# A four-layer graph network on one core: scatter signals by half groups, later passes that use a chunk inside the next one's products, destination rows projected first

## The reference, cut to what matters

```python
# layer 0, twice: messages, gated update
agg = segment_sum(concat(h[src], h[dst]) @ W_msg.T + b_msg, dst)
gi, gh = agg @ W_ih.T + b_ih, h @ W_hh.T + b_hh
r, z = sigmoid(ir + hr), sigmoid(iz + hz); n = tanh(inn + r * hn)
h = where(deg > 0, (1 - z) * n + z * h, h)
# layer 1: weighted sum over edges, both ends normalised by degree
out = segment_sum(norm[:, None] * (h @ W)[src], dst) + b
# layer 2: attention per feature
e = leaky_relu((h @ W_src.T + b_src)[src] + (h @ W_dst.T + b_dst)[dst])
out = segment_sum((h @ W_v.T + b_v)[src] * edge_softmax(e, dst), dst)
# layer 3: mean over neighbours
h1 = relu(h @ W1 + b1); neigh = segment_sum(h1[src], dst) / max(deg, 1)
out = relu(relu(h1 @ W_self + neigh @ W_neigh + b_sage) @ W2 + b2)
```

## Time and profile before

| | us |
|---|---|
| median of 3 runs (lowest, highest) | 3011.63 (3008.87, 3012.08) |
| profiled execution, its own time | 3001.93 |
| its span | 3000.2 |
| scatters on POOL | 70.9 to 1085 |
| rest of unzip and first pass | 1085 to 1266 |
| pass 1 | 1266 to 1436 |
| pass 2 | 1461 to 1664 |
| to attention | 1664 to 1731 |
| attention | 1731 to 2749 |
| layer 3 with pass 3 | 2749 to 3000 |

### The profile page before, as it was taken

How to read it: one execution, slowest core, us unless ns; L and a number is a source line. 1 busy time by engine, 2 the same in 40 slices (tenths; PEclk the granted TensorE clock), 3 DMA queues, 4 the chain that set the end, 5 groups by cost and what they waited for, 6 DMA issues and landing times.

```text
span 3000.2 us, 36506 instructions
## 1 busy us (share of the span) xinstructions
PE 2037.3 (68%) x11168; PEld 1241.8 (41%) x11322; DVE 1720.4 (57%) x2673; ACT 977.4 (33%) x1778; POOL 1619.1 (54%) x1664
## 2 busy tenths in 40 slices
PE   4774006251615056899798389999999999994597
PEld 2222001021302024555444267666666666663244
DVE  7997412121212023535225279999999999997622
ACT  1000003120202020101200157777777777774101
POOL 1777777777777730020000467777777777775000
PEclk8555557665757578899999789999999999997799
DMA  9998979481835096442585389999999999995252
GB/s 388 375 367 320 366 255 393 171 294 30 291 121 187 3 304 191 145 154 68 204 284 165 110 249 314 313 309 304 301 316 310 313 307 310 312 306 180 88 177 64
DMA packets 496975, 724.17 MB, mean 241 GB/s; under 512 B 70532, under 2 KB 353725, under 8 KB 496880
## 3 DMA queue, kind: packets, MB, share of 16 engines
q1 hardware_dynamic: 425316, 608.72, 60.8%
q0 software_dynamic: 65680, 109.05, 12.3%
q10 hardware_dynamic: 5884, 5.21, 0.5%
HBM read 402.27 MB, written 320.51 MB: 241 GB/s over the span
## 4 chain that ended last, share of the span: by engine, by line
PE 31%; POOL 30%; issue 14%; DMA 12%; DVE 10%; ACT 1%; SPq 0%; POOLq 0%; DVEq 0%; ACTq 0%; another core or an unknown queue 0%
POOL adj_d L578 21%; POOL G L572 9%; DMA G<-tab_sv,src_e 8%; PE PS L911 7%; PE PS L920 5%; PE PS L647 3%; DMA G<-adj_d 3%; PE PS L941 2%; PE PS L936 2%; PE PS L966 2%; PE PS L781 2%; DVE V L1505 2%; PE PS L935 1%; DVE V L1504 1%; POOL run_d L616 1%
## 5 line engine op out<-in xcount | busy, mean ns | idle before, releaser
L578 POOL DMA_INDIRECT adj_d<-D,place x782 | 775.8, 992 | 303.2 <-issue 237.8
L572 POOL DMA_INDIRECT G<-tab_sv,src_e x784 | 758.8, 968 | 245.7 <-issue 220.0
L935 PE MATMUL PS<-ident,G 128*128 128x128 f32 x784 | 219.0, 279 | 110.1 <-DMA G<-tab_sv,src_e 63.4
L936 PE MATMUL PS<-VT 128*128 128x128 f32 x1568 | 274.9, 277 | 0.0
L1810 DVE TENSOR_TENSOR_SCAN RB<-mring,RB,PS 128x512 f32<-128x512 bf16 x196 | 249.3, 1272 | 23.9 <-PE PS L941 20.2
L1284 ACT ACTIVATE X<-G 128x512 f32<-128x512 f32 x150 | 98.8, 668 | 500.6 <-DMA G<-adj_d 500.6
L1790 DVE TENSOR_TENSOR_SCAN HTx<-PS,HTx,D 128x512 f32<-128x512 f32 x196 | 250.2, 1276 | 0.0
L1795 DVE TENSOR_TENSOR_SCAN ST<-PS,ST,M 128x512 f32<-128x512 f32 x196 | 250.0, 1276 | 0.0
L936 PEld LDWEIGHTS PS<-VT 128*128 128x128 f32 x1568 | 243.3, 196 | 0.0
L616 POOL DMA_INDIRECT run_d<-V,head_i x25 | 24.0, 959 | 382.3 <-ACT V L1354 375.0
L1175 ACT ACTIVATE OSF<-PS 128x512 f32<-128x512 f32 x392 | 209.9, 587 | 5.1 <-PE PS L647 3.8
(11 more groups left out here) (393 smaller groups left out, 4230.3 us busy)
## 6 DMA issues: line engine op xcount, KB each, us to landing
frac_d<-OSF SPq DMA_DIRECT2D x196, 512.0 KB
adj_d<-RB SPq DMA_DIRECT2D x7, 12800.0 KB, 74.1
G<-adj_d SPq DMA_DIRECT2D x162, 512.0 KB, 6.3
run_d<-RB SPq DMA_DIRECT2D x4, 12992.0 KB, 81.7
VT<-run_d SPq DMA_DIRECT2D x196, 256.0 KB
wts_d<-X SPq DMA_DIRECT2D x150, 256.0 KB, 6.5
mring<-cut_d SPq DMA_DIRECT2D x196, 128.0 KB
HTx<-seg_d SPq DMA_DIRECT2D x196, 128.0 KB
```

Source lines behind the costliest of these rows:

```text
L572: pool.indirect_dma_start(dest, None, table, bass.IndirectOffsetOnAxis(ap=idx, axis=0)).then_inc(done, 16)
L578: pool.indirect_dma_start(adj_d, bass.IndirectOffsetOnAxis(ap=place[:, 2 * w + k:2 * w + k + 1], axis=0), pay[:, w, k, :], None).then_inc( ...
L935: nc.tensor.matmul(o, G[:, h, k, 0:F], ident[:, :], is_transpose=True, start=k == 0, stop=False, skip_group_check=True)
L936: last = nc.tensor.matmul(o, GZ[:, h, k, :], HM[:, q, k * P:(k + 1) * P], start=False, stop=False, skip_group_check=True)
```

## The change

Four edits.

1. The scatter goes in 46 units of 9 and 8 windows in place of 23 groups of 17. In step u: writes k = 0 of unit u; wait for the k = 1 writes of unit u - 2 and `gdn` up; wait for the k = 0 writes of unit u - 1; its k = 1 writes. `gate_i` counts units.
2. Chunk 5 is unzipped in two pieces of 256 columns, as chunk 6 was, with two blocks to a load: 26 loads for 25. The work for earlier chunks goes with the first piece.
3. In the later passes chunk s - 1 is turned behind the fourth tile of chunk s and folded behind its twentieth, and its `after` comes at the end of chunk s. Behind the last chunk one turn, one fold and one `after` are left. ScalarE and VectorE follow. In pass 1, where only 5 tiles are left of chunks 0 and 1 in order, the turn stands behind the fourth of them and the fold behind the fifth.
4. Before attention the transposes of a group alternate with the product of its destination rows (128 columns), which ScalarE evicts at once; the source and value tables (256 columns) are a second round. SP stores all of `tab_d` before `tab_sv`. `MEV_L3` counts the 14 evictions.

```diff
-PIECES = [(j, 0, CW) for j in range(6)] + [(6, 0, 256), (6, 256, LASTC)]
+PIECES = [(j, 0, CW) for j in range(5)] + [(5, 0, 256), (5, 256, CW), (6, 0, 256), (6, 256, LASTC)]
-LOADS = [(i, b, 1 if j < 6 else min(2, NBR - b)) for ... for b in range(0, NBR, 1 if j < 6 else 2)]
+LOADS = [(i, b, 1 if j < 5 else min(2, NBR - b)) for ... for b in range(0, NBR, 1 if j < 5 else 2)]
+UW = (9, 8)
+NU = 2 * NSG
...
                 pool.wait_ge(gated, 1)
-                for g in range(NSG + 1):
-                    if g < NSG:
...
-                        for w in range(g * GW, (g + 1) * GW):
...
-                            issue(0, g, w)
-                    if g >= 1:
-                        landed(0, g - 1)
-                        for w in range((g - 1) * GW, g * GW):
-                            issue(1, g - 1, w)
-                    if g >= 2:
-                        landed(1, g - 2)
...
+                    for w in windows(u):
...
+                        issue(0, u, w)
+                    if u >= 2:
+                        landed(1, u - 2)
                         pool.sem_inc(gdn, 1)
...
+                    if u >= 1:
+                        landed(0, u - 1)
+                        for w in windows(u - 1):
+                            issue(1, u - 1, w)
...
             def dense_pass(d, tile, after, early=0):
-                for s in range(NCH + 3):
...
+                for s in range(NCH):
+                    first = early if s < 2 else 0
+                    if s >= 2:
+                        pe.wait_ge(xev, NCH * d + s - 1)
+                    for b in range(first, NBR):
+                        tile(s, b, PS[:, 4 + s % 2, 0:CWD(ORDER[s])])
+                        if s >= 1 and b == first + 3:
+                            turned(s - 1)
+                        if s >= 1 and b == max(first + 4, 19):
+                            nodes(s - 1)
+                    if s >= 1:
+                        after(ORDER[s - 1])
+                turned(NCH - 1)
+                nodes(NCH - 1)
+                after(ORDER[-1])
...
-            for g in range(NG):
-                pe.wait_ge(hg, NG + g + 1)
-                turn_group(lambda b: H[:, b, :], g)
-            pe.wait_ge(tre, state["tr"])
...
+            for g in range(NG + 1):
+                if g < NG:
+                    pe.wait_ge(hg, NG + g + 1)
+                    turn_group(lambda b: H[:, b, :], g)
+                if g >= 1:
+                    pe.wait_ge(tre, TRE_L2 - NG + g)
+                    if g >= 3:
+                        pe.wait_ge(mev, MEV_L2 + g - 2)
+                    rows(g - 1).then_inc(mm, 1)
...
-            product(qkv)
+            product(table)
...
             def dense_pass(d, after):
-                for s in range(NCH + 3):
-                    if 1 <= s <= NCH:
-                        hots(NCH * d + s - 1, ORDER[s - 1])
-                        split_columns(NCH * d + s - 1)
-                    if s >= 3:
-                        after(ORDER[s - 3])
+                for s in range(NCH):
+                    hots(NCH * d + s, ORDER[s])
+                    split_columns(NCH * d + s)
+                    if s < NCH - 2:
+                        after(ORDER[s])
+                after(ORDER[NCH - 2])
+                after(ORDER[NCH - 1])
```

More of the change, by code:

```diff
@@ L450, in unzip_pass @@
                     if b == 0:
[L451 removed]
+                        sp.wait_ge(gdn, sp.value_load(gate_i[0:1, NSG + i:NSG + i + 1], min_val=1, max_val=NU) if i + 1 < len(PIECES) else NU)
                     if n >= 3:
@@ L602, in scatter, with windows, issue, landed @@
-                landed(1, NSG - 1)
-                pool.sem_inc(gdn, 1)
+                def windows(u):
+                    w0 = u // 2 * GW + u % 2 * UW[0]
+                    return range(w0, w0 + UW[u % 2])
+                def issue(k, u, w):
+                    pool.indirect_dma_start(adj_d, bass.IndirectOffsetOnAxis(ap=place[:, 2 * w + k:2 * w + k + 1], axis=0), pay[:, w, k, :], None).then_inc(sgr[k][u % 2], 16)
+                def landed(k, u):
+                    pool.wait_ge(sgr[k][u % 2], 16 * UW[u % 2] * (u // 2 + 1))
@@ L605, in last_sums @@
+                landed(0, NU - 1)
+                for w in windows(NU - 1):
+                    issue(1, NU - 1, w)
+                for u in (NU - 2, NU - 1):
+                    landed(1, u)
+                    pool.sem_inc(gdn, 1)
             def last_sums():
@@ L876, in dense_pass, with turned, nodes @@
             def dense_pass(d, tile, after, early=0):
-                for s in range(NCH + 3):
[L880 to L884, removed]
-                    if 1 <= s <= NCH:
[L886 to L896, removed]
-                    if s >= 3:
-                        after(ORDER[s - 3])
+                def turned(s):
+                    pe.wait_ge(xev, NCH * d + s + 1)
+                    if s >= 1:
+                        pe.wait_ge(xrd, NCH * d + s)
+                    if d == 1 and s == 0:
+                        pe.wait_ge(lasts, 1)
+                    turn_columns(ORDER[s])
+                def nodes(s):
+                    pe.wait_ge(xrd, NCH * d + s + 1)
+                    pe.wait_ge(ohd, NCH * (d + 1) + s + 1)
+                    pe.wait_ge(aev, NCH * (d - 1) + s)
+                    fold(NCH * d + s, ORDER[s], acc)
+                for s in range(NCH):
[8 more added lines that the diff above has]
+                            nodes(s - 1)
+                    if s >= 1:
+                        after(ORDER[s - 1])
+                turned(NCH - 1)
+                nodes(NCH - 1)
+                after(ORDER[-1])
             def counts(d, take, order):
@@ L1147, in take_agg @@
             def take_agg(d, cols, raw, after):
-                for s in range(NCH + 3):
+                for s in range(NCH + 1):
+                    if s >= 1:
+                        j = ORDER[s - 1]
+                        if s == NCH:
+                            after(ORDER[s - 2])
+                        act.wait_ge(acc, NCH * (d - 1) + s)
+                        nc.scalar.activation(cols[:, j * CW:j * CW + KB(j) * P], PS[:, 7, 0:KB(j) * P], ACT.Copy).then_inc(aev, 1)
                     if s < NCH:
@@ L1275, in turned, with weights @@
                     state["tr"] += 1
-                def weights(j, groups):
-                    for g in groups if j < 6 else ():
-                        for n in range(j * NBR + 4 * g, j * NBR + 4 * g + KB(g)):
+                def weights(i, groups):
+                    for n, (i_, b, nb) in enumerate(LOADS[:NWT]):
+                        if i_ == i and b // 4 in groups:
+                            w = nb * (PIECES[i][2] - PIECES[i][1])
                             act.wait_ge(tld[n % 3], 16 * (n // 3 + 1))
@@ L1345, in _ @@
             ln_sqrt(3)
-            take(groups(HT))
+            for s in range(NG + 1):
+                if s < NG:
+                    take(groups(HT)[s:s + 1])
+                if s >= 1:
+                    act.wait_ge(mm, state["mm"] + 1)
+                    nc.scalar.activation(V[:, 4 * (s - 1):4 * (s - 1) + KB(s - 1), :], PS[:, 6 + (s - 1) % 2, 0:KB(s - 1) * P].rearrange("p (k f) -> p k f", f=F), ACT.Copy).then_inc(mev, 1)
+                    state["mm"] += 1
             for g in range(NG):
@@ L1930 @@
 MEV_L2 = NG
+MEV_L3 = 3 * NG
 TRE_R1 = 8 + 2 * NG
```

110 lines of the change are left out of this document (58 added, 52 removed).

## The result

The changed kernel takes 2916.19 us (median of 4 runs, 2913.77 to 2917.72), the kernel before 3010.25 in the same comparison (4 runs, 3003.8 to 3012.08). The ratio is 0.9694, 95% interval 0.9677 to 0.9710: 94.1 us less. Forecast were 2918 us and 94 less. The profiled execution took 2915.68 us, its span is 2913.9, so in the profiles 86.3 us are gone, not 94: the profiled execution of before was 8.3 us faster than its median, that of after 0.5.

What follows compares the result with a forecast made beforehand. The kernel was taken as a row of stages, the largest share, 21%, POOL issuing the scatter. -83 + 1 + 7 - 12.5 + 0 - 6.4 = -93.9, say -94, from the median 3011.6: 2918 us, range 2897 to 2957.

Steps and rivals of the forecast that it cites:

- Scatter tail, -83: End of scatter and unzip: earlier signals and smaller pieces put the last copy at 1121.6 in place of 1204.7, 83 us less.
- My cover of 14 us: Last piece of chunk 6: gates keep VectorE busy to 1103, past the signal at 1089, so the last wait costs nothing.
- The stall: Unzip of chunk 5: VectorE waited 18.3 us for one load; if only in the profiled execution, 15 us were never winnable.
- the rival built on it: Unzip of chunk 5: timed runs never had the 15 us wait for a load, so 2933 us; chance 0.25.
- POOL waits, +1: Scatter on POOL: 23 more landing waits cost an issue gap at most, 1 us added (0 to 7).
- rival: slower, 0.03: Scatter on POOL: each of 46 units waits for landings; at 15 us a landing, 3130 us; chance 0.03.
- Pass 1, +7: Pass 1: TensorE waits 1.6 us at four folds, 2.8 in the second chunk, 3.5 at the end; 7 us more (+3 to +13).
- Pass 2, -12.5: End of pass 2: two VectorE updates left instead of three, normalisation at 1650.7 against 1663.2; 12.5 us less (-10 to -14).
- Pass 3, 0: Pass 3: nothing waits inside, end keeps a split and an eviction of idle; no change (-2 to +2).
- Rows first, -6.4: Before attention: normalisation to POOL's first head scatter takes 6.4 us in place of 12.8; 6.4 us less (-4 to -8).
- Tail bound by loads: Unzip: chunk 5's halves run late, chunk 6 opens at 1080 or so, 24 us less gained, 2942 us; chance 0.12.
- no gain: Unzip: the pieces gain nothing, only -12 us would be left, 3000 us; chance 0.03.

Runs made afterwards that it cites:

- edit 1 alone: Changed kernel with later passes and order before attention taken back, half groups and chunk 5's split kept: 2921.32 us, ratio 0.9733; on a slow chip 1.0024.
- pass 1 old: Changed kernel with pass 1 alone in the order of the kernel before: 2908.35 us, ratio 0.9673 to the kernel before; slow chips 0.9990 and 0.9981.
- full groups: Changed kernel with scatter units of 17 windows, chunk 5 still in two pieces: 2931.48 us, ratio 0.9770 to the kernel before; on a slow chip 0.9990.

## Why the prediction was right, point by point

**Scatter tail, -83: mechanism right, 7.6 us too much (1129.2 for 1121.6).** The pieces opened as worked out from units, columns and 1.30 us a scatter, each 3 to 4.4 us late: 906.4, 994.0 and 1059.1 for 902, 990 and 1056. One term that was off is "its stretch is unchanged work, 60.6 us". It is the same work, but before it began with three loads in hand: 3.1 us. The first copy came at 1063.3 for 1061, 2.3. The landing of the last scatters was the other: I took 4 us, from head scatters in a quiet stretch and from scatters under way in the fills, and 10.4 as worst; it is 15.9 (16.3 in edit 1 alone, and 1106.0 - 1089.7 = 16.3 with pass 1 old). My cover of 14 us held all of it but 1.3, and 0.8 behind: 2.1. (The 16 us that the sum has ahead of the 1056 signal are 1056 - 1038 = 18; nothing hangs on it.)

**The stall was no one-off, and the rival built on it (2933, 0.25) falls.** All five profiles of fast chips have it: loads stuck until 1104.5 in the kernel before (last scatter 1083.9) and until 1104.2 with full groups (1086.5); a landing of 16 us in the other three. So it is likely that the kernel before lost its 15 us in chunk 5 in its timed runs too; the change puts the stall where only the last piece waits for it, under the gates. In the changed kernel the last packets of the scatter's queue are gone at 1093.5 and none of any queue moves until the load at 1105.8: it is not bandwidth. (The Trainium skill, DMA: Bandwidth & Descriptors, section Anatomy of one DMA — SWDGE (gpsimd) path, has some 2.0 us as the fixed part of a transfer; by that, an estimate, the last piece would have opened near 1092. The trace has 15.9 us here, so the measurement decides.)

**POOL waits, +1 (rival: slower, 0.03).** Right: landings cost POOL 2.4 us in 8 gaps. The last scatter is nevertheless 5.9 us later, outside the 5 that I had allowed: 0.9 is a later start, and the mean scatter took 999 ns for 992, 782 x 0.007 = 5.5 us. Attention's gathers, which no edit touches, have 972 for 968. With full groups the line of the earlier trace rows is at 954/958 again, with edit 1 alone too, and its end at 1091.1. So the pace differs by some tenths of a per cent from execution to execution, and the half groups cost between nothing and 2.4 us: first to last scatter takes 1015.8 to 1018.0 with them, 1015.6 without.

**Pass 1, +7: right in each wait (four of 1.58, one of 2.33, one of 3.10 for 1.6, 2.8 and 3.5), 3.3 short in the sum.** The waits and the small gaps beside them come to 6.9 for 5.7, and the clock to 3.4 where the rounding up from 5.7 to 7 left it 1.3. That is the term that was mis-sized. I had 13 as the bound with half clock behind each wait; of the new waits it came behind one, that of 2.33 us in the second chunk, and behind none of the four of 1.58. +10.3 lies in the range but above the 5 to 9 that I had named as the sign of being right, and the old order gives 8.6 back (10.3 by the profile of edit 1 alone).

**Pass 2, -12.5: -12.1**, and 10 to 13 on the slow chip as well. **Pass 3, 0: 0.1.** **Rows first, -6.4: -6.4** to attention's first product, the last tenths by luck: the head scatter comes 7.0 us behind normalisation where the sum had 6.4 (the 1.7 us for bias, eviction and semaphore were 0.6 short), so the edit itself brings 5.8, and the other 0.6 passed between there and attention's first product, by what no row says.

**The total, 2918 for 2916, is better than its terms, by luck.** In the profiles the errors come to +7.6 us (POOL and tail together +6.5, pass 1 +3.3, passes 2 and 3 +0.5, the untouched stages -2.8); they are made up by the 8 us by which the profiled execution of before lay below the median of its runs. In the three other comparisons on fast chips before is 3000.6, 3002.1 and 3005.8, so a median of 3010 to 3012 was on the high side, and 94 us may be some us too much; the changed kernel was not timed on those chips.

**Tail bound by loads (0.12; 0.03 for no gain).** Not so: the last copies of chunk 5's halves are at 953 and 1026, 41 and 33 us before the next piece opened.

## What to carry to other kernels

A consumer that waits for a whole chunk of a producer's output should wait for the part it reads: here finer signals and a split of the one chunk that was waited for were worth 81 us alone; the reordering of pass 2 and of the projections brought 12 and 6 in the profiles, and that of pass 1 took 10. The gain exists only while the signal is what ends the wait: when something ahead of the consumer is later (here the merging, on three chips), it is zero, so look for the next releaser before counting it. And a reordering that is right where VectorE's chain is shorter than the products ahead of the fold (pass 2, at most 15.1 us against 17.2) can be wrong where it is longer (pass 1, 15.1 against 13.5): choose by pass. The mixed order has the shortest profile, though its ratio and that of the changed kernel are not apart.

## What the runs showed of the hardware

- The landing of the last indirect writes of a long row came 15.9 to 16.3 us behind their issue in three profiles, 12 to 13 us behind the last packet of any queue; transfers under way at that time stood as long (13.7 and 18.3 us of idle on VectorE). In these five profiles the end of the stall fits both the end of the scatter (16.0 to 20.6 us behind it) and the time since its first write (1032 to 1034 us), the second range being the narrower. Against the second speak the runs without twelve units, whose loads move some 400 GB/s in just that time, but on slow chips and in a shorter scatter; the run was to part the two and could not. The cause stays open.
- A signal of POOL comes earlier than its place between POOL's rows: with full groups the piece at 1028.6 opened when by the rows (34 scatters of 1.27 us ahead of 1086.5) it stood at 1043, 15 us or 11 scatters on. This fits a POOL that goes on to its wait ahead of its rows, so that only the landing holds the signal; the wait itself has no row. The prediction's count of scatters left (144, 76, 25) leans on the same thing without saying so: it puts the signal ahead of the 8 or 9 writes that stand in front of it in the code.
- The same kernel took 3001 to 3010 us on some chips and 3944 to 3957 on others, steady on each, by waits between TensorE and VectorE that no row explains.
